# Sixteen gate products made one product and sixteen transfers, and three narrow evictions opened to a second engine, in a 12-block diffusion transformer kernel

## What is computed

```python
x = L0(x, cond, ctx)   # blocks 0, 1 "rope" (16 heads of 64, turned by angles), 2 "ff"
x = L1(x, cond, ctx)   # blocks 3, 4 "small" (16 heads of 8), 5 "ff"
x = L2(x, cond, ctx)   # blocks 6, 7 "flat" (16 heads of 64), 8 "ff"
x = L3(x, cond, ctx)   # blocks 9, 10 "small", 11 "ff"
...
# L3, where the gates are
mod = silu(c) @ adaln_w.T + adaln_b
shift_sa, scale_sa, gate_sa, shift_ca, scale_ca, gate_ca, shift_ff, scale_ff, gate_ff = split(mod, 9)
h = modulate(ln(x), shift_sa, scale_sa)
q = ln(heads(h)) * qn_w + qn_b;  k = ln(heads(h)) * kn_w + kn_b;  v = heads(h)
x = x + gate_sa[:, None, :] * unheads(softmax(q k^T * scale) v)
h = modulate(ln(x), shift_ca, scale_ca)          # block 10: cross attention
x = x + gate_ca[:, None, :] * (attention(h, kv) @ ca_out_w.T + ca_out_b)
h = modulate(ln(x), shift_ff, scale_ff)          # block 11
x = x + gate_ff[:, None, :] * (silu(h @ w1.T) * (h @ w3.T) @ w2.T)
```

## Time and profile before

| what | value |
|---|---|
| median of 3 executions | 1471.23 us (1471.11 to 1471.91) |
| profiled execution | 1467.77 us, span 1466.0 us |
| PE busy | 1394.7 us (95%) |
| DVE busy | 1306.7 us (89%) |
| ACT busy | 1153.1 us (79%) |
| POOL busy | 860.3 us (59%) |
| mean granted TensorE clock | 0.991 |

### The profile page before, as it was taken

One profiled execution on the slowest core, in us unless ns is written; L12 is line 12 of the kernel. 1 busy time (PEld: TensorE's weight loads), 2 busy tenths in 40 slices (PEclk: granted clock), 3 DMA queues, 4 the chain that ended last, 5 costly groups with the idle time before them and its releaser, 6 DMA issues.

```text
span 1466.0 us, 40764 instructions
## 1 busy us (share of the span) xinstructions
PE 1394.7 (95%) x15176; PEld 1165.7 (80%) x15176; DVE 1306.7 (89%) x3601; ACT 1153.1 (79%) x4946; POOL 860.3 (59%) x981
## 2 busy tenths in 40 slices
PE   6999999999989999999999999999999999999887
PEld 6788778888767878888888878788878888888755
DVE  7998889899999898987898999999998888989797
ACT  2567899698676788888899857777889879878585
POOL 5556675346576775455556475866685545445553
PEclk9999999999999999999999999999999999999988
DMA  9300000000000000000000000000000000000000
GB/s 291 132 2 2 2 2 2 2 2 4 10 8 4 8 2 2 2 2 2 2 2 6 10 8 2 7 9 8 2 2 2 2 2 2 2 2 4 2 5 7
DMA packets 15222, 20.66 MB, mean 14 GB/s; under 512 B 4400, under 2 KB 11568, under 8 KB 15024
## 3 DMA queue, kind: packets, MB, share of 16 engines
q1 hardware_dynamic: 13328, 14.32, 3.2%
q10 hardware_dynamic: 1696, 3.72, 0.7%
HBM read 16.99 MB, written 1.05 MB: 12 GB/s over the span
## 4 chain that ended last, share of the span: by engine, by line
PE 66%; DVE 20%; ACT 10%; issue 1%; POOL 1%; ACTq 0%; DMA 0%; SPq 0%; POOLq 0%; DVEq 0%
PE ps L784 13%; PE ps L908 11%; ACT E L998 8%; PE ps L949 6%; PE ps L935 6%; PE ps L800 6%; DVE negmax L1303 5%; PE ps L810 4%; PE ps L871 4%; PE ps L960 3%; PE ps L885 3%; PE ps L922 3%; PE ps L898 3%; DVE E L1466 2%; DVE E L1369 1%
## 5 line engine op out<-in xcount | busy, mean ns | idle before, releaser
L998 ACT ACTIVATE E<-ps,negmax 128x128 f32<-128x128 f32 x2048 | 727.1, 425 | 62.6 <-DVE negmax L1303 62.1
L1146 POOL TENSOR_TENSOR E<-E,rinv 128x512 f32<-128x512 f32 x450 | 470.6, 1055 | 219.9 <-DVE rinv L1312 217.7
L998 ACT ACTIVATION_READ_ACCUMULATOR E<-ps,negmax 128x1 f32 x2048 | 536.0, 265 | 0.0
L1303 DVE TENSOR_REDUCE negmax<-ps 128x4 f32<-128x512 f32 x512 | 331.2, 679 | 35.3 <-PE ps L871 15.0
L908 PE MATMUL ps<-consts,E 128*128 128x128 f32 x2048 | 295.4, 279 | 15.1 <-POOL E L1146 6.2
L908 PEld LDWEIGHTS ps<-consts,E 128*128 128x128 f32 x2048 | 232.8, 143 | 72.9 <-POOL E L1146 30.8
L1036 ACT ACTIVATE E<-ps 128x512 f32<-128x512 f32 x251 | 152.1, 632 | 93.9 <-PE ps L908 93.4
L1466 DVE COPY E<-ps 128x512 f32<-128x512 f32 x261 | 175.2, 680 | 14.7 <-PE ps L908 13.4
L1139 POOL TENSOR_TENSOR E<-E,prod 128x512 f32<-128x512 f32 x122 | 156.0, 1286 | 52.3 <-DVE prod L1372 45.4
L1085 POOL TENSOR_TENSOR rstd<-ve,consts 128x1 f32<-128x1 f32 (+1 forms) x192 | 109.3, 574 | 115.6 <-DVE ve L1256 105.6
L1117 POOL TENSOR_TENSOR xb<-X,rows 128x128 f32<-128x128 f32 x120 | 54.9, 459 | 140.9 <-DVE X L1214 112.5
(11 more groups left out here) (155 smaller groups left out, 2765.8 us busy)
## 6 DMA issues: line engine op xcount, KB each, us to landing
w_f<-res_f SPq DMA_DIRECT2D x6, 256.0 KB, 9.8
w_cq<-res_cq SPq DMA_DIRECT2D x2, 512.0 KB, 9.8
w_co<-res_co SPq DMA_DIRECT2D x2, 512.0 KB, 13.3
w_f<-res_f SPq DMA_DIRECT2D x2, 512.0 KB, 7.4
out_x<-X SPq DMA_DIRECT2D x16, 64.0 KB, 1.5
E<-in_x SPq DMA_DIRECT2D x15, 64.0 KB, 1.8
w_ck<-res_ck SPq DMA_DIRECT2D x2, 384.0 KB, 10.7
w_cv<-res_cv SPq DMA_DIRECT2D x2, 384.0 KB, 11.9
```

Of the source, the lines that this page charges most:

```text
L998: last = nc.scalar.activation(E[p][:, h, :], bank(u, j * N, (j + 1) * N), ACT.Exp, bias=negmax[p][:, h:h + 1], accum_out=sums[p][:, h:h + 1])
L1146: tt(e, e, rinv[p][:, T4 * g:T4 * g + T4].unsqueeze(2).broadcast_to([N, T4, N]), ALU.mult).then_inc(done[POOL], 1)
L1303: nc.vector.tensor_reduce(negmax[p][:, T4 * g:T4 * g + T4], bank(u).rearrange("p (h m) -> p h m", h=T4), AX, ALU.max, negate=True).then_in ...
```

## The change

Gates. One product per kernel instead of sixteen: silu(c) of all samples (128x16) is stationary and the same 128x384 weights move, so the bank holds sixteen rows of three gates. VectorE adds the bias to these 16x384 numbers in a new tile `gate_rows`. SyncE writes that tile to a DRAM tensor `all_gates` once, waits for it, and then sends each sample its row, repeated to 128 partitions, into the same `gates` as before, when the sample's sum of block 7 is done. `gb` and the three gated sums wait for that transfer instead of for VectorE.

Evictions. `Q` and `V` of the small blocks and `HC` may be done by VectorE or ScalarE, as the planner decides for each. ScalarE's `V` waits for VectorE's `K` (both read one bank).

Tables. The planner's numbers (`AGE`, `TURN`, `AHEAD`, `LEAN`, `FAVOUR`, `KEEP`) are others; `AHEAD` has no entry for small scores any more. So the whole order is another.

```diff
-AGE = 14.8
-TURN = [0, 0, 0, -4, -4, 2, 5, -3, 7, 1, 0, -3, 0, -8, 13, 24]
-AHEAD = {"small": 9.3, "flat": 4.8}
+AGE = 13.8
+TURN = [0, 0, -7, -4, -4, 2, 5, -3, 7, 0, -10, -3, -3, -8, 13, 24]
+AHEAD = {"flat": 4.0}
...
-    (POOL, "RK", "rope"): -4, (POOL, "gb", "small"): 96, (POOL, "power", "flat"): -2, (POOL, "power", "rope"): 40,
+    (POOL, "RK", "rope"): -16, (POOL, "power", "ff"): -2, (POOL, "power", "small"): -12,
...
-            add(PE, "G", 0.65, (PE, "T"), fills=("G",))
-            add(DVE, "G", 0.46, (PE, "G"), empties="G")
+            if s == 0:
+                add(PE, "G", 0.65, fills=("G",))
+                add(DVE, "G", 0.46, (PE, "G"), empties="G")
...
+    if KIND[b] == "small" and step in ("Q", "V", "HC"):
+        return {DVE: 0.24 if step == "Q" else 0.2, ACTE: 0.25}
...
+        gate_rows = sb("gate_rows", S, 3 * D)
+        all_gates = nc.dram_tensor("all_gates", (S, 3 * D), fp32, kind="Internal").ap()
...
+                elif step == "sum" and b == L3_SELF - 2:
+                    p = s % STREAMS
+                    if not all_out:
+                        all_out.append(s)
+                        sp.wait_ge(done[DVE], DONE[DVE, "G", L3_SELF, 0])
+                        sp.dma_start(all_gates, gate_rows[:, :]).then_inc(gates_out, 16)
+                        sp.wait_ge(gates_out, 16)
+                    count = DONE[DVE, "sum", b, s]
+                    if fresh(sp, done[DVE], count):
+                        sp.wait_ge(done[DVE], count)
+                    sp.dma_start(gates[p], all_gates[s].partition_broadcast(128)).then_inc(gates_loaded[p], 16)
...
-                    mm(bank(u, 0, 3 * D), siluT[:, s:s + 1].broadcast_to([128, N]), wt[:, :],
-                       start=True, stop=True).then_inc(done[PE], 1)
+                    mm(ps[0:S, u[0], 0:3 * D], siluT[:, :], wt[:, :], start=True, stop=True).then_inc(done[PE], 1)
...
+                if step == "V" and b != L3_SELF:
+                    count = DONE[DVE, "K", b, s]
+                    if fresh(act, done[DVE], count):
+                        act.wait_ge(done[DVE], count)
...
+                    nc.scalar.activation(own_features[p], bank(u, at, at + D).rearrange("p (j r e) -> p r j e", r=T4, e=HD),
+                                         ACT.Copy).then_inc(done[ACTE], 1)
+                elif step == "HC":
+                    nc.scalar.activation(hc[p], bank(u, 0, N), ACT.Copy).then_inc(done[ACTE], 1)
...
-                tt(gates[p], bank(u, 0, 3 * D), row("g0", 3), ALU.add).then_inc(done[DVE], 1)
+                    tt(gate_rows[:, :], ps[0:S, u[0], 0:3 * D], row("g0", 3)[0:S, :], ALU.add).then_inc(done[DVE], 1)
```

84 lines of the change are left out of this document (51 added, 33 removed).

## The result

| | median us | ratio to before, 95% interval |
|---|---|---|
| before | 1471.11 | |
| changed | 1480.24 | 1.0063 (1.005 to 1.0076) |

What follows compares the result with a forecast made beforehand. TensorE was taken to set the pace (66% of the chain), VectorE close behind (20%). Span 1466.0 - 8.0 + 1.8 - 1.8 = 1458.0, 1459.8 with the 1.8 us around it, median 3.5 higher: 1463.3 us, range 1453 to 1474.

Steps and rivals of the forecast that it cites:

- The gate products: Fifteen of sixteen removed, 0.70 us of TensorE each, 10.5 us in all; gain taken as 8.0 us, between 5.6 and 10.5.
- the lower bound of the gain, if the rest of the path stayed as it is: Eight gate products and one eviction on the chain, less the product left: 5.84 + 0.44 - 0.70 = 5.6 us.
- At 20% of the chain: Fifteen gate evictions leave VectorE, 8.1 us in all, priced by VectorE's 20% share of the chain at 1.6 us gained.
- 66% of 10.5: TensorE's 10.5 us of removed gate products, priced by its 66% share of the chain at 6.9 us gained.
- The transfers: SyncE's gate transfers land within 6.0 us for the first, 4.5 us after, under 54 us of cover: cost nothing.
- The narrow evictions: `Q` to VectorE, `V` and `HC` to ScalarE at 350 ns; nothing waits, cost nothing, -2 to +2 us for both.
- The wide evictions and the tables: VectorE some 5 us more in all, priced +1.0 us; six more table changes on ScalarE, 7.7 us, priced +0.8 us.
- The new order: Order of all steps chosen anew: -1.8 us, called a choice and not a reading, with bounds -8 and +12.
- Rival 3: VectorE ends last in rope blocks, given 20.9 us more: 1476.2 us, range 1474 to 1480; chance 0.12.
- Rival 2: Gain given back where VectorE is as full as TensorE and by a clock fall near the end: 1468.3 to 1474; chance 0.15.
- Rival 1: New order gives 6 us more as transposes' weight loads wait under 20 us for GpSimd: 1450 to 1459; chance 0.17.
- Rival 4: Gates come late and the sums of block 9 wait, 6 us against 54 us of cover; no chance of its own.

Runs made afterwards that it cites:

- the run of the gates alone: Kernel before with its order, engines and tables kept; only fifteen gate products struck out, gates from one product and sixteen transfers: 1469.17 us, ratio 0.999.
- giving way: GpSimd instructions wait for the VectorE step they held: 34 in the changed kernel, 1463.85 us; 25 in the before order with one gate product, 1459.61 us.

## Why the prediction was wrong

The forecast was 1463.3 us in 1453 to 1474, faster with 0.73; the time is 1480.2. In the prediction's terms, -8.0 us for the gates and nothing in sum for all else; by the runs -1.5 for the gates and +10.7 for all else.

**The gate products: the term that failed first.** -8.0 us, in 5.6 to 10.5, by counting eight of the sixteen on the chain. Measured alone: -1.5 us, at most -3.4. What one occupies was right (0.64 us at the place shown, 0.64 to 0.75 by the prediction), though TensorE's busy time fell by 8.0 us and not by 15 x 0.70 = 10.5; what fills the rest isn't shown. The step that failed is "the lower bound of the gain, if the rest of the path stayed as it is". A chain that ended last tells what was last, not by how much: a second path, through VectorE, ScalarE or GpSimd by the place, ran less than 0.7 us behind at eleven of the fifteen. At two more the start 0.7 us earlier met a GpSimd instruction (0.83 us lost) and the lower clock came one stretch of ten us earlier (1.9 us lost for a while). "At 20% of the chain" and "66% of 10.5" failed for the same reason; shares of a chain are no prices where four engines are 79 to 95% busy. The sign that the prediction named for its own failure, that TensorE's idle time grows by as much as the products gave, is what the run of the gates alone shows (+8.5 us).

**The transfers: right.** Nobody waits for them in the changed kernel; they land in 3.0 us. Where the cover was missing, for the first transfer in the run of the gates alone, GpSimd waited 3.4 us, under the 6.0 us of the estimate, and some 0.5 us of it reached the path.

**The narrow evictions: duration right, "nothing waits" wrong.** 350 ns was taken for the copy on ScalarE in 277 to 405, and it is 306. "So nothing waits" looked at the reader `MX` alone: ScalarE itself waits 8.9 us for VectorE's `K` before these copies. Whether that costs time isn't shown; taking the choice back costs 7 to 9 us, in an order made for it.

**The wide evictions and the tables: one sum and the places wrong.** VectorE's busy time was to grow by 0 to 8 us and grew by 11.5, and 9.0 of these 11.5 are holds: over their quiet durations VectorE's SBUF steps take 46.6 us too long, before 37.6. The priced part is thus 2.5 us. ScalarE is 2.3 us up where 3 to 10 less was said: that sign leaves out the prediction's own 7.7 us of table loads, with which its 8 us less come to nothing. Table loads were priced by amount, 6 x 1.283 us at 10%, +0.8; it is their place, behind a wait of ScalarE at 4 points against 1, that cost 4 to 5.5 us.

**The new order: the term that turned the sign.** "-1.8 us for a new order" was called a choice and not a reading; its bound above was +12, and the order came out near it. By the runs: changed less gates alone is 0.0073, 10.7 us. Of that the table loads are 4.0 to 5.5, and the difference between what giving way brings in the two orders is 15.5 - 9.1 = 6.4. Together 10.4 to 11.9: within the doubt of such sums of ratios, 3 to 4 us, nothing of size is left over. With both taken out, the new order is level with the old one or a little ahead (0.9922 and 0.9904 against 0.9934 and 0.9928).

The cause of the holds was in the trace of before: a norm of mean 377 ns among quiet ones of 338, second parts of gated sums of 292 ns that took 1055. The prediction read none of these rows, and said that GpSimd's and VectorE's durations are unchanged by an order. They are not. The planner's own list of steps that wait for GpSimd says so in the code of the kernel before.

**The rivals.** Rival 3 came nearest to the time, 1474 to 1480, and has half its signs: VectorE's share rose, to 25% and not 30, and TensorE is idle in the rope stretches (5.7 us more from 850 to 1100 us). Its deciding one is missing: VectorE has 25% of the chain from 350 to 550 us and 36% from 850 to 1100, not over 40% (before: 37% and 24%). And its cause, the 20.9 us of evictions moved to VectorE, is not needed: with all of them still on VectorE and the holds gone, VectorE's share is 19%, under the 20% of before, and the loss is gone. Rival 2 is what happened to the gates' term: the gain is given back, one place of it by the clock that the rival named, in the run of the gates alone. In the changed kernel the clock is no cause of the loss: its mean is 0.992, against 0.991 before. In the stretches of ten us near its end one has 0.68 and the others 0.83 or more; the kernel before has one at 0.66 there and the others at 0.83 or more too, not the three or four at 0.6 to 0.8 of which the prediction speaks. Two falls further ahead are new (0.83 from 410 to 420 us, 0.85 from 1110 to 1120):

```profile
1420.00:1430.00 10.00, 7.11 (x57) 5.47 (x57) 8.73 (x26) 5.67 (x27) 8.06 (x7) 0.68 0.01 2
1430.00:1440.00 10.00, 8.47 (x82) 5.64 (x85) 9.15 (x23) 7.77 (x37) 4.50 (x6) 0.97 0.00 0
```

Rival 1 is out by its own sign: the transposes wait 39.2 us for GpSimd, not under 20. Rival 4 doesn't apply.

**Left open.** Why a held step on the chain returns about 70% and not all: GpSimd's delay of 0.3 to 0.6 us each and the next path that ends last both take from it, and the runs don't part them. What the narrow evictions bring in an order that doesn't depend on them wasn't tried.

## What to carry to other kernels

Before pricing work that a change takes away, ask what is second: where a fixed order runs several engines at 80 to 95%, a product taken from a gap gives nothing, or a loss further on, and one run with the order frozen and that work struck out tells so. When VectorE and GpSimd both work in SBUF, compare the mean of each short VectorE operation with its minimum; where the mean is higher, look in order of time for the GpSimd instruction beside it, above all where a VectorE step that releases GpSimd is followed at once by an SBUF-only step. Let GpSimd wait for that second step: at the place shown it cost GpSimd 0.3 us and saved VectorE 0.9. The remedy fits one order and its trace; a planner's rule for such holds should be checked against the trace in the same way, since the one here foresaw a gain of 5 us. And put a dummy of the next function ahead of ScalarE's wait, where a table load falls behind one.
